# Side work placed by the time that the attention leaves on TensorE, in a kernel of two attentions and two FFNs

## The reference, cut to what matters

```python
# x: (8, 1024, 256) float32
x = x + attn_a(layernorm(x))   # one distance map for all heads
x = x + ffn(layernorm(x))
x = x + attn_b(layernorm(x))   # 16 heads of width 16, queries times keys
x = x + ffn(layernorm(x))

# attn_a
V = x @ wv.T + bv;  pos = x @ w3d.T + b3d          # three coordinates a token
scores = -dist(pos, pos) * scale                   # causal, softmax over keys
out = softmax(scores) @ V;  return out @ wo.T + bo
# ffn
xr, xk = mixes of x and of x one token earlier
return sigmoid(xr @ W_r.T) * (relu(xk @ W_k.T) ** 2 @ W_v.T)
# attn_b
k, q, v = split(x @ Wkqv + b);  softmax(causal(q @ k.T / 4)) @ v
```

## Time and profile before

| | us |
|---|---|
| median of 3 runs (lowest, highest) | 2317.15 (2314.3, 2317.2) |
| the profiled execution | 2316.06 |
| its span, first to last instruction | 2314.3 |
| TensorE busy | 1929.1 |
| VectorE busy | 1417.5 |
| ScalarE busy | 1254.3 |
| GpSimd busy | 1024.2 |

### The profile page before, as it was taken

How to read it: one execution, slowest core, us unless ns; L and a number is a source line. 1 busy time by engine, 2 the same in 40 slices (tenths; PEclk the granted TensorE clock), 3 DMA queues, 4 the chain that set the end, 5 groups by cost and what they waited for, 6 DMA issues and landing times. The chain is left out here.

```text
span 2314.3 us, 32515 instructions
## 1 busy us (share of the span) xinstructions
PE 1929.1 (83%) x9842; PEld 936.3 (40%) x9842; DVE 1417.5 (61%) x4173; ACT 1254.3 (54%) x2673; POOL 1024.2 (44%) x1074
## 2 busy tenths in 40 slices
PE   4477888888988899788987889888887889988986
PEld 3344343334433354324543345333443335432423
DVE  2336677567676666666765666756656666677642
ACT  0623654675537555394545755366554855555563
POOL 4454354335642455334743266423654246422414
PEclk8677899989998899989999899998999899999998
DMA  3006011310132111211122011231113111141100
GB/s 96 0 20 117 1 28 42 69 28 15 43 85 34 28 29 53 67 29 28 33 67 64 13 29 37 76 63 28 28 37 83 28 28 28 43 87 29 29 19 19
DMA packets 64347, 97.27 MB, mean 42 GB/s; under 512 B 15655, under 2 KB 58029, under 8 KB 58030
## 3 DMA queue, kind: packets, MB, share of 16 engines
q1 hardware_dynamic: 64174, 95.20, 18.6%
HBM read 61.09 MB, written 33.55 MB: 41 GB/s over the span
## 5 line engine op out<-in xcount | busy, mean ns | idle before, releaser
L852 ACT ACTIVATE pt<-exp_bank 128x512 f32<-128x512 f32 (+3 forms) x1536 | 742.5, 494 | 806.5 <-PE exp_bank L822 797.0
L867 DVE CUSTOM_DVE_ANT_0 max_bank<-max_bank,mask 128x128 f32<-128x128 f32 (+3 forms) x1024 | 500.3, 502 | 495.2 <-PE max_bank L811 478.2
L822 PE MATMUL exp_bank<-qs,ks 98*128 98x512 bf16 (+3 forms) x1536 | 523.8, 347 | 72.5 <-ACT pt L852 66.3
L811 PE MATMUL max_bank<-ks,qs 96*128 96x512 bf16 (+3 forms) x1536 | 525.0, 349 | 24.3 <-DVE piece_max L870 17.2
L870 DVE TENSOR_REDUCE piece_max<-max_bank 128x1 f32<-128x512 f32 x512 | 342.9, 686 | 164.7 <-PE max_bank L811 161.5
L837 PE MATMUL o_bank<-pt,v 128*17 128x512 f32 (+3 forms) x3072 | 346.2, 525 | 8.0 <-ACT pt L852 3.0
L889 POOL TENSOR_SCALAR_AFFINE_SELECT pt<-pt 128x512 f32<-128x512 f32 x256 | 170.1, 664 | 404.2 <-ACT pt L852 403.8
L353 POOL TENSOR_SCALAR xh<-xs,mv,rstd 128x256 f32<-128x256 f32 x256 | 322.6, 1266 | 10.0 <-PE side L379 3.8
L822 PEld LDWEIGHTS exp_bank<-qs,ks 98*128 98x128 bf16 x1536 | 153.9, 101 | 353.4 <-ACT pt L852 229.5
L811 PEld LDWEIGHTS max_bank<-ks,qs 96*128 96x128 bf16 x1536 | 154.7, 101 | 257.9 <-issue 102.1
L544 PE MATMUL side<-vp,p 128*128 128x260 f32 x576 | 185.2, 450 | 33.7 <-ACT p L473 18.3
(11 more groups left out here) (94 smaller groups left out, 2243.0 us busy)
## 6 DMA issues: line engine op xcount, KB each, us to landing
parts_dram<-parts SPq DMA_DIRECT2D x64, 384.0 KB, 2.6
qs<-parts_dram SPq DMA_DIRECT2D x192, 128.0 KB, 7.0
ks<-parts_dram SPq DMA_DIRECT2D x32, 384.0 KB, 4.8
xs<-in_L_attn_a_x_dram SPq DMA_DIRECT2D x16, 512.0 KB, 4.3
ks<-parts_dram SPq DMA_DIRECT2D x32, 256.0 KB, 5.5
out_dram<-xs SPq DMA_DIRECT2D x16, 512.0 KB, 3.1
ks<-parts_dram SPq DMA_DIRECT2D x32, 128.0 KB, 5.9
qs<-neg_maxT SPq DMA_DIRECT2D x64, 8.0 KB, 1.9
```

The lines of the kernel that those rows point to most:

```text
L811: pe.matmul(max_bank[u % MAX_BANKS][:, 0:k1 - k0], qs[r][0:KROWS, j, P * tile:P * (tile + 1)], ks[r][0:KROWS, j, k0:k1], start=True, stop= ...
L822: pe.matmul(exp_bank[k % EXP_BANKS][:, 0:q1 - q0], ks[r][:, j, P * kt:P * (kt + 1)], qs[r][:, j, q0:q1], start=True, stop=True).then_inc(s ...
L852: act.activation(pt[:, e % 2, j, 0:q1 - q0], exp_bank[k % EXP_BANKS][:, 0:q1 - q0], ACT.Exp, scale=SCALE).then_inc(exp_done, 1)
L867: dve.tensor_tensor_reduce(scores, scores, mask[:, HALF - w:HALF], 1.0, LOWEST, ALU.add, ALU.max, piece_max[:, j, m:m + 1]).then_inc(max_f ...
```

## The change

The plan is made in ticks and no longer in quarters. `attention_time(u)` gives the columns that the attention of quarter u takes on TensorE, `LEFT` what remains of 2,700 columns (300 at least), and `TICK` the running sum, scaled so that a group of 48 quarters has 48 ticks. `moment(tick)` turns a tick into a quarter, with a fraction that orders several ticks in one quarter. `place()` walks through ticks, one part each; starts, due times and the emptying of banks are ticks. `schedule()` now writes the steps of a quarter in the order of their moments.

The constants change with it: att1, ffn2, ffn4 and proj3 start at -46, 35, 75 and 112 instead of -44, 50, 82 and 114; the second halves of att1 and of the FFNs start 12 and 20 ticks after the first instead of 8 and 16, that of proj3 10 instead of 12. Jobs stand further apart: values of att1 two ticks instead of one, projections four instead of three, keys, receptance and products three or four instead of two; the values of proj3 have their two parts one tick apart instead of three quarters. The pieces of the distances get 6, 4, 3 and 3 ticks for 512, 384, 256 and 128 columns instead of 6, 5, 4 and 3. Where one generator wrote all of att1's steps on an engine in a fixed order, there are now two or three, each by its own due times.

```diff
 QUARTERS = 4 * SLOTS
 TURN = 4 * NS
-ATT1, FFN2, FFN4, PROJ3 = -44, 50, 82, 114
-FIRST = {("att1", 0): -220, ("ffn2", 0): -126, ("proj3", 0): -74,
-         ("att1", 1): -28, ("ffn2", 1): 66, ("proj3", 1): 114}
+ATT1, FFN2, FFN4, PROJ3 = -46, 35, 75, 112
+FIRST = {("att1", 0): -240, ("ffn2", 0): -154, ("proj3", 0): -88,
+         ("att1", 1): -36, ("ffn2", 1): 50, ("proj3", 1): 112}
 OUTPUT_AT = [4 * (LEAD + TPH + 1) + 1, 4 * (LEAD + NP + 1) + 1]
-LN_HALF = {"att1": 8, "ffn2": 16, "ffn4": 16, "proj3": 12}
+LN_HALF = {"att1": 12, "ffn2": 20, "ffn4": 20, "proj3": 10}
...
-PIECE_TIME = [2 + (q1 - q0) // P for _, q0, q1 in KEY_PIECES] + [5, 5, 5]
-PIECE_AT = [34 + sum(PIECE_TIME[:p]) for p in range(NP + 4)]
+PIECE_TIME = [max(3, 1 + 5 * (q1 - q0) // HALF) for _, q0, q1 in KEY_PIECES] + [5, 5, 5]
+PIECE_AT = [32 + sum(PIECE_TIME[:p]) for p in range(NP + 4)]
...
-        "att1": [("values1", t, 16 + t + TPH * (t // TPH), 1, 1, 2) for t in range(NT)] +
-                [("positions", k, 29 + k, 1, 1, 1) for k in range(6)] +
+        "att1": [("values1", t, 16 + 2 * t + TPH * (t // TPH), 1, 1, 2) for t in range(NT)] +
+                [("positions", k, 26 + k + 7 * (k // 3), 1, 1, 1) for k in range(6)] +
                 [("attend", t, PIECE_AT[attended_from(t)] + 2, t // 2 + 1, 1, 2) for t in range(NT)],
-        "ffn": [("keys", j, 24 + 2 * j, 2, 1, 1) for j in range(2)] +
-               [("receptance", j, 31 + 2 * j, 2, 1, 1) for j in range(2)] +
-               [("products", j, 36 + 2 * j, 2, 1, 2) for j in range(2)],
-        "proj3": [("project", j, 24 + 3 * j, 2, 1, 1) for j in range(8)] +
-                 [("values3", j, 26 + 6 * j, 2, 3, 2) for j in range(4)]}
+        "ffn": [("keys", j, 24 + 3 * j, 2, 1, 1) for j in range(2)] +
+               [("receptance", j, 30 + 4 * j, 2, 1, 1) for j in range(2)] +
+               [("products", j, 37 + 3 * j, 2, 1, 2) for j in range(2)],
+        "proj3": [("project", j, 24 + 4 * j, 2, 1, 1) for j in range(8)] +
+                 [("values3", j, 26 + 4 * j, 2, 1, 2) for j in range(4)]}
...
+def attention_time(u):
+
+    t, j = divmod(u, GH)
+    width = [k1 - k0 for _, k0, k1 in QUERY_PIECES][t % NP] + [q1 - q0 for _, q0, q1 in KEY_PIECES][(t - LEAD) % NP]
+    return width + (4 * ([q1 - q0 for _, q0, q1 in KEY_PIECES][(t - LEAD - 1) % NP] + 64) if j == GH - 1 else 0)
...
+LEFT = [max(2700 - attention_time(u), 300) for u in range(GH * NP)]
+TICK = [0]
+for u in range(QUARTERS + 200):
+    TICK.append(TICK[-1] + LEFT[u % (GH * NP)] * GH * NP / sum(LEFT))
...
+def moment(tick):
+
+    if tick < 0:
+        return tick
+    u = next(u for u, at in enumerate(TICK) if at >= tick - 1e-6)
+    first = next(k for k in range(tick, -2, -1) if k < 0 or u > 0 and TICK[u - 1] >= k - 1e-6)
+    return u + (tick - first - 1) / 8
...
-    free, before, shift, u = [BEGIN, BEGIN], BEGIN, 0, BEGIN
+    free, before, shift, tick = [BEGIN, BEGIN], BEGIN, 0, BEGIN
     while parts or rows:
-        while rows and rows[0][0] <= u and min(free) <= u:
+        u = moment(tick)
+        while rows and rows[0][0] <= u and min(free) <= tick:
             key = rows.pop(0)[1]
             k = free.index(min(free))
-            quarters[key], bank[key], emptied[key] = [u], k, u + 2
-            free[k] = u + 2
+            quarters[key], bank[key], emptied[key] = [u], k, moment(tick + 2)
+            free[k] = tick + 2
         if parts:
             at, key, k, last = parts[0]
             regained = max(0, shift - max(0, at - before) // 4)
-            if at + regained <= u and (k > 0 or min(free) <= u):
+            if at + regained <= tick and (k > 0 or min(free) <= tick):
                 parts.pop(0)
-                before, shift = at, max(regained, u - at)
+                before, shift = at, max(regained, tick - at)
...
-                    emptied[key] = free[bank[key]] = u + delay[key]
-        u += 1
+                    free[bank[key]] = tick + delay[key]
+                    emptied[key] = moment(tick + delay[key])
+        tick += 1
...
-    WRITTEN_AT[k] = max(k + max(0, shift - (k - since) // 4), WRITTEN_AT.get(k - 1, BEGIN))
+    WRITTEN_AT[k] = max(moment(k + max(0, shift - (k - since) // 4)), WRITTEN_AT.get(k - 1, BEGIN))
...
-        def dve_att1(at, n):
+        def dve_values1(n):
...
+        def dve_distances(at, n):
...
+                yield at(PIECE_AT[p + 1])
...
+        def dve_residuals(n):
...
+                yield EMPTIED_AT["attend", "att1", n, 0, t]
...
-        def act_att1(at, n):
+        def act_positions(n):
...
+        def act_distances(at, n):
...
-        def pe_att1(n):
+        def pe_values1(n):
...
+        def pe_positions(n):
...
+        def pe_attend(n):
...
-                yield at(17 + c)
+                yield at(16 + c)
...
-                yield at(28 + 2 * j)
+                yield at(28 + 3 * j)
...
-                yield at(41 + 2 * j)
+                yield at(42 + 3 * j)
...
-                yield at(21 + c)
+                yield at(19 + 2 * c)
...
-                yield at(23 + 2 * c)
+                yield at(25 + 2 * c)
...
-                yield at(24 + 3 * j + 3)
+                yield at(24 + 4 * j + 3)
...
-                for entry in parts:
-                    while entry[0] <= u:
-                        entry[0] = next(entry[1], NEVER)
-                parts = [entry for entry in parts if entry[0] < NEVER]
+                while parts and (first := min(parts, key=lambda entry: entry[0]))[0] < u + 1:
+                    first[0] = max(first[0], next(first[1], NEVER))
+                    if first[0] == NEVER:
+                        parts.remove(first)
```

97 lines of the change are left out of this document (44 added, 53 removed).

## The result

The changed kernel takes 2338.1 us in the median (2336.1 to 2343.8, 4 runs), the kernel before 2315.7 (2311.4 to 2317.2, 4 runs): 1.0104 of it, 95% interval 1.0080 to 1.0127. The forecast was 2341. The profiled execution after took 2339.05 us, its span 2337.3.

What follows compares the result with a forecast made beforehand. ScalarE was taken to bound each turn's first 57 us, PE with its side-bank waits the rest. Six turns of (4 + 1 - 1), first turn +3, prologue -3 gave +24: 2341 us, range 2258 to 2385.

Steps and rivals of the forecast that it cites:

- Reuse of the banks: Side matmuls waiting for one of two side banks to be emptied: +4 us a turn (+1.7 to +9.9).
- counting rule: Side-bank waits a turn: jobs reusing a bank in its emptying quarter, one later or later still, times 0.72, 0.23, 0.08 us.
- PE's clock: In ScalarE's stretch, granted 0.79, it could rise with more side work; worth little, not in the sum.
- Lumps: Side work heaped in fourth quarters, empty quarters behind, PE waiting on VectorE's maxima: +1 us a turn (0 to 5.7).
- Distances: ScalarE's stretch: squeezed from 60 to 56 quarters, FFN work 15 quarters earlier, four exponentials leave: -1 us a turn (-2 to 0).
- Prologue: Before the first maxima matmul: first squares about 4 us earlier, projections and position jobs +1 each: -3 us (-5 to +1.5).
- First turn: Second batch's distances all ahead of the first exponentials, ScalarE gets about 7 us more before quarter 56: +3 us (0 to +5).
- Last turn and tail: End of the kernel: the same chain in both orders, 0 us.
- A: Rival, faster: wider spacing removes waits before values and projections, 8.4 us a turn: 2267 us, chance 0.37.
- B: Rival: lumps cost in full, starving ScalarE in its stretch too, empty quarters not caught up: 2405 us, chance 0.11.
- C: Rival: nothing measurable, waits only move between lines, +1 to +4 us: 2319 us, chance 0.12.
- Turns of 277 us, times six: Middle turns, one of 273 us standing for six of eight, each growing by 4 + 1 - 1 us: +24.

Runs made afterwards that it cites:

- only_distances: room_ticks_old_constants with one changed constant, the distances squeezed from 60 to 56 quarters: 2348.4 us, 1.0130 of the kernel before.
- room_ticks_old_constants: The changed kernel with all constants, spacings and stage starts of the kernel before; ticks by room and split streams stay: 2312.7 us, 0.9993 of the kernel before.
- before_distances66: The kernel before with the distances of a batch stretched from 60 to 66 quarters, nothing else: 2336.0 us, 1.0106 of the kernel before.
- dist_att1_proj: only_distances plus the changed spacings of the first attention's values and positions, projections and third values: 2347.4 us, 1.0102 of the kernel before.

## Why the prediction came out right, and where it was not

The total was right (+22 measured, +24 forecast); its terms were only in part, and that they summed to it was partly luck: the largest loss that the experiments found, the distances, stood in the sum as a gain, and what took most of it back had no term.

- *Reuse of the banks, +4 a turn.* Right in sign, mis-sized: the idle time before side matmuls rose by 8.8 us (25.8 to 34.6; said 28 to 32), near the upper end of +9.9. The counting rule behind it fails as a predictor, as the prices 0.64 to 1.21 show, and only_distances lost 36 us with one same-quarter reuse less than its pair (28, 29).
- *PE's clock.* No term stood for it; the prediction called it worth little. PE's busy time in the turn went from 235.5 to 230.7 us, -4.8, which took back over half of the added waits. The turn is the sum of both: idle +8.1, busy -4.8, together +3.3. For the same work, PE's busy time in the fifth turn runs from 223.0 to 239.0 us over the kernels. The Trainium skill, TensorE: Matmul & The Clock Gate, section Why this matters for your kernels, asks for TensorE kept busy continuously. The traces agree between two side banks and three, where both fell (changed kernel with two maxima banks: idle 44.4 to 24.7 us, busy 239.0 to 227.6); they don't between the kernels before and after, where idle time rose and busy time fell. The prediction had cited it and priced it at nothing; why the changed kernel's clock was the better one is not shown.
- *Lumps, +1.* No loss: room_ticks_old_constants is at 0.9993. The reading that late placement is a flaw fails where it was tested: undoing it costs 48 us with three side banks.
- *Distances, -1.* The step that failed. It reckoned the stretch as ScalarE's work alone, took four exponentials out and called PE's share outside. The first group was to shorten by 1 to 2 us and grew by 3.4. Done alone, the squeeze costs 6.9 us in the first group, gives back 1.3 in the second, 36 us in all. In the stretch PE then does 20 products more, at 442 ns each instead of 411. The earlier FFN starts, in the same term, cost up to 25 more with the halves. What hid both in the total is the FFN spacing with its due times, -34 us, for which the sum had no term; most of that lies in the prologue and the first two turns.
- *Prologue, -3.* The first squares do come earlier (54.23 us instead of 59.57), and yet the first maxima matmul starts 1.1 us later (209.3; said 205). Why the gain is lost on the way was not tested.
- *First turn, +3.* Its first group took 3.6 us more (37.6 against 34.0), as said; the rest of the turn gave it back and more (232.4 against 233.2 us).
- *Last turn and tail, 0.* The tail took 4.1 us more, by the clock.
- *Rivals.* A's mechanism is partly real (L534 5.0 to 1.3 us), but what it freed was taken by products, positions and maxima. B is out: the waits before maxima and scores fell, 11.0 to 9.9. C is out: the interval, 1.0080 to 1.0127, is clear of 1.
- *Turns of 277 us, times six.* 276.3 for the turn shown, made of +8.8 in side waits, -0.7 in the other idle time and -4.8 in busy time. But six turns did not each get +4: from the second to the seventh they got -4.9, +2.1, +4.8, +3.4, +2.9 and +8.6, +16.9 in all instead of +24. The tail, the first maxima matmul and the last turn made up the rest. One turn stood for six less well than the prediction took it to; why the seventh got most was not tested.

## What to carry to other kernels

Count a matmul engine's time as idle plus busy at the clock that the order earns, and read the two together: here they moved the same way in some pairs of plans and against each other in others. When one table of numbers is changed at several places, look where each entry puts the first dependent matmuls (into another engine's stretch, or beside the next stage's transposes), and not only at how much work it moves; here, on one path, four groups of entries were worth +36, 0, +25 and -34 us. Cut the difference by turns before explaining it from one: of the -34, the turn shown holds 1.9. Before moving work about to avoid waits for two buffers, ask whether a third can be had: one PSUM bank taken from where three were held gave 7%, while no order of the jobs with two gained anything that could be measured.

## What was unexpected of the hardware

In only_distances the granted clock fell to 1.2 GHz by the end of three waits of 1.04, 0.49 and 1.00 us among small matmuls, and four matmuls of 260 columns then took 2.10 us instead of 1.04; in before_distances66 it stayed at 2.4 GHz behind a single wait of 2.44 us (four of them in 1.14 us). With three side banks PE needed 223.0 us for a turn's matmuls where the kernel before needs 235.5, 5% less, with nothing changed in them. And one of six runs of one plan (dist_att1_proj) took 2315 us and the others 2344 to 2351; what it did differently has no profile and stays open.
